# Linear attention with two gated networks: the low-half subtraction behind the state sums, and the out-projection written product by product

## The reference

```python
def linear_attention(x, Wq, Wk, Wv, Wo, out_norm_w):   # 8 heads of 128, chunks of 128 tokens
    def step(S, qkv):
        qb, kb, vb = qkv
        attn = jnp.einsum('bhid,bhjd->bhij', qb, kb)
        attn = jnp.where(causal, attn, 0.0)
        o = jnp.einsum('bhij,bhjv->bhiv', attn, vb) + jnp.einsum('bhid,bhdv->bhiv', qb, S)
        S = S + jnp.einsum('bhid,bhiv->bhdv', kb, vb)
        return (S, o)
    ...
    o = rmsnorm(o, out_norm_w)
    return o @ Wo
...
s = xn + linear_attention(rmsnorm(xn), ...)
s = s + silu(rmsnorm(s) @ Wgate) * (rmsnorm(s) @ Wup) @ Wdown
g = silu(fp4_network(xn))          # gate, up and down with 4-bit rounding in groups of 16
return x + s * g
```

## Time and profile before

| | us |
|---|---|
| median of 3 runs | 1060.57 |
| lowest, highest | 1059.28, 1060.98 |
| the profiled execution | 1059.62 |
| its span | 1057.9 |

### The profile page before, as it was taken

The page is one execution under the profiler, slowest core; times in us unless marked ns, Lnnn a source line. Parts: engine busy times, 40 slices in busy tenths (PEclk is TensorE's granted clock), DMA queues, the critical chain, the costliest instruction groups (busy, mean ns, idle before and its releaser), DMA issues.

```text
span 1057.9 us, 18981 instructions
## 1 busy us (share of the span) xinstructions
PE 1048.9 (99%) x6790; PEld 959.9 (91%) x6790; DVE 891.3 (84%) x1860; ACT 558.4 (53%) x1604; POOL 47.3 (4%) x68
## 2 busy tenths in 40 slices
PE   9999999999999999999999999999999999999998
PEld 6899999989999999998999989999999999999997
DVE  6788888888887888887777898889888888888887
ACT  6765765756757657667666634343333333333332
POOL 1000000000000000000000000101011010101010
PEclk9999999999999999999999999999999999999999
DMA  6555355455463553654446522253423233323213
GB/s 219 170 166 177 115 168 161 139 158 167 140 191 127 179 179 118 186 161 148 159 132 195 163 84 81 81 159 100 129 76 120 89 117 100 121 86 100 81 59 111
DMA packets 166238, 143.10 MB, mean 135 GB/s; under 512 B 28800, under 2 KB 162944, under 8 KB 166144
## 3 DMA queue, kind: packets, MB, share of 16 engines
q1 hardware_dynamic: 165456, 141.88, 43.2%
q10 hardware_dynamic: 688, 0.00, 0.0%
HBM read 77.27 MB, written 64.57 MB: 134 GB/s over the span
## 4 chain that ended last, share of the span: by engine, by line
PE 89%; DVE 4%; DMA 3%; ACT 2%; issue 1%; SPq 1%; DVEq 0%; ACTq 0%
PE ps L263 70%; PE ps L726 5%; PE ps L772 4%; PE ps L778 4%; PE ps L756 4%; DMA r_gate<-moved 1%; DMA moved<-work 1%; PE ps L861 1%; PE ps L614 0%; DMA work<-kept_w 0%; SPq L417 0%; DVE work L1406 0%; DMA work<-in_L_attn_hidden_states 0%; ACT work L996 0%; ACT work L969 0%
## 5 line engine op out<-in xcount | busy, mean ns | idle before, releaser
L263 PE MATMUL ps<-r_k,r_gate_up 128*128 128x512 f32 x768 | 185.2, 391 | 0.0
L263 PEld LDWEIGHTS ps<-r_k,r_gate_up 128*128 128x128 f32 x768 | 141.5, 188 | 27.2 <-DVE work L1654 0.4
L263 PE MATMUL ps<-r_o,onT 128*128 128x256 f32 x768 | 106.8, 288 | 0.0
L263 PE MATMUL ps<-r_h,r_k 128*128 128x512 f32 (+1 forms) x393 | 105.2, 403 | 0.0
L263 PEld LDWEIGHTS ps<-r_q,r_v 128*128 128x128 f32 x768 | 99.7, 191 | 4.9 <-DVE r_v L1658 0.3
L263 PE MATMUL ps<-r_q,r_v 128*128 128x256 f32 x768 | 102.3, 283 | 0.0
L969 ACT ACTIVATE work<-ps 128x128 f32<-128x128 f32 x256 | 67.1, 278 | 59.4 <-PE ps L778 59.2
L263 PE MATMUL ps<-r_h,r_q 128*128 128x512 f32 x384 | 98.2, 391 | 0.0
L263 PE MATMUL ps<-r_v,r_h 128*128 128x512 f32 x384 | 97.4, 390 | 0.0
L263 PEld LDWEIGHTS ps<-r_o,onT 128*128 128x128 f32 x768 | 95.7, 190 | 0.2
L1165 ACT ACTIVATE r_v<-work 128x512 fp32r<-128x512 f32 x64 | 40.5, 633 | 99.7 <-DVE work L1654 99.6
(11 more groups left out here) (161 smaller groups left out, 2049.3 us busy)
## 6 DMA issues: line engine op xcount, KB each, us to landing
moved<-work SPq DMA_DIRECT2D x63, 512.0 KB, 2.9
r_gate<-moved SPq DMA_DIRECT2D x252, 128.0 KB, 2.5
kept_h<-work SPq DMA_DIRECT2D x31, 384.0 KB, 2.6
work<-kept_h SPq DMA_DIRECT2D x124, 96.0 KB, 2.3
work<-in_L_attn_hidden_states SPq DMA_DIRECT2D x15, 512.0 KB, 5.1
kept<-work SPq DMA_DIRECT2D x9, 514.0 KB, 4.3
kept_h<-work SPq DMA_DIRECT2D x9, 512.0 KB, 3.5
kept_xq<-work SPq DMA_DIRECT2D x8, 512.0 KB, 5.4
```

The source lines that it names most:

```text
L263: done = pe.matmul(out_ap, a, b, start=first and n == 0, stop=last and n == 2, skip_group_check=skip)
```

## The change

On VectorE `o_lo` moves from ahead of the state sums to behind them, ahead of `late_extras`; only the very last step keeps its order. On TensorE the out-projection no longer goes chunk by chunk with three products each, but product by product with the four chunks each: high x high, then low weight x high activation, then high weight x low activation. It waits for `onT_hi` at its start and for `onT_ready` ahead of the last four matmuls.

```diff
@@ out_projection, tensor block
-                    pe.wait_ge(onT_ready, value)
-                    for c in range(CH):
-                        done = split_product(pe, ps[:, B_Y + c // 2, (c % 2) * D:(c % 2 + 1) * D],
-                                             lambda a: wo[:, a, h, :], lambda a: onT[:, a, c * P:(c + 1) * P],
-                                             "activation stationary", h == 0 and c % 2 == 0,
-                                             h == H - 1, skip=True)
+                    pe.wait_ge(onT_hi, value)
+                    for n, (wp, ap) in enumerate(((HI, HI), (LO, HI), (HI, LO))):
+                        if ap == LO:
+                            pe.wait_ge(onT_ready, value)
+                        for c in range(CH):
+                            done = pe.matmul(ps[:, B_Y + c // 2, (c % 2) * D:(c % 2 + 1) * D],
+                                             onT[:, ap, c * P:(c + 1) * P], wo[:, wp, h, :],
+                                             start=h == 0 and n == 0 and c % 2 == 0, stop=h == H - 1 and n == 2,
+                                             skip_group_check=True)
@@ attention, vector block
                     early_extras(b, j, mine)
                     if final and j == STEPS - 1:
                         last_o_lo(t0 + j - 1)
-                    elif not first or j >= LAG:
-                        o_lo(t0 + j - 1)
                     dve.wait_ge(ds_done, t0 + j + 1)
...
                         last = to
+                    if (not first or j >= LAG) and not (final and j == STEPS - 1):
+                        o_lo(t0 + j - 1)
                     late_extras(b, j, mine)
```

## The result

The changed kernel takes 1062.44 us (median; 1060.90 to 1064.59), the kernel before, in runs beside it, 1060.58 (1059.08 to 1062.86). The ratio of the two, formed from the means of these runs, is 1.0021 with a 95% interval of 1.0014 to 1.0028: slower, by 1.9 us from median to median and by 2.2 us from mean to mean. The interval lies on both sides of 0.2%, so the case is on the border between "within 0.2%" and "slower". The profiled execution took 1063.78 us, its span 1062.0.

A forecast was written before the change was run, and what follows sets the result against it. TensorE, busy 99% of the span, was taken as the bound, so only its standstills could be won. Gains of 1.95 us and losses of 3.3 gave +1.35, forecast 1061.9 us, range 1059.0 to 1064.0.

The forecast's parts named there:

- b1 j5: Batch 1, step 5 (steps 0 to 15, batches 0 to 3): sums start earlier without the subtraction ahead, 0.57 us won.
- b3 j4: Batch 3, step 4: TensorE's wait of 0.79 us for the sums shortened, 0.6 us won.
- b3 j12: Batch 3, step 12: the subtraction waiting for ScalarE's rounding no longer holds the sums, 0.58 us won.
- b0 j13: Batch 0, step 13: eight loads back from 1.18 to 0.97 us, 0.2 us won.
- b3 j14: Batch 3, step 14: counted at nothing, since VectorE then waits for ScalarE and a DMA; bounds 0 and 0.48 us won.
- Loss (a): j = 0 into j = 1, batches 1 to 3: VectorE 0.6 us late, all reaching TensorE; 1.8 us lost.
- Loss (b): j = 3 of each batch: next hidden state's low half late for the scores; 0.6 + 3 x 0.3 = 1.5 us lost.
- The price: VectorE time of the moved subtraction per step, start to next start: 0.6 us, bounds 0.57 and 0.69.
- full-duration rival: Subtraction costs its full duration, 0.69 us, and ScalarE's queue falls behind too: 1062.9 us, chance 0.22.
- Product order: TensorE's out-projection product by product: costed at nothing, 0.8 us either way; rival with its own price 1061.1 or 1062.7, chance 0.08.
- The ninth pair: Out-projection pair first needing the low half, ready 0.35 us before wanted; rival that it waits: 1065 us, chance 0.05.
- that lateness: VectorE's work after the moved subtraction, up to 0.6 us later; claimed never to add up, and hidden outside two step kinds.

The follow-up runs named there:

- the last experiment: Sums first only in j = 1, 5, 12, 13, 14, ScalarE's rounding behind the first state in j = 1; 1059.33 us against 1061.72 for the kernel before, ratio 0.9974.
- e2: Changed kernel, but in j = 0 of each batch the low-half subtraction stays ahead of the sums; 1061.75 us against 1060.95 for the kernel before, ratio 1.0002.
- e1: Kernel before with only the out-projection changed to product by product, the subtraction staying ahead of the sums; 1060.89 us against 1060.95, ratio 0.9996.
- e4: Changed kernel with the sums first only in j = 4, 5, 12, 13, 14; 1060.53 us, ratio 0.9994 to the kernel before.

## Why the prediction was right, and where it was not

**What bounds the kernel.** Right. The same instructions with gaps in other places give the whole difference.

**Gains.** The places were right, and so was the mechanism: no group at line 781 waits for the sums at b1 j5, b3 j4 and b3 j12 (the prediction had left a wait of about 0.2 at the first two). The size at the first two was too small, 0.57 and 0.6 where the table has 0.82 each. In the first profile of before, VectorE had waited for the exchange DMA at the transposed k of the same steps too, 0.54 at b1 j5 and 1.51 at b3 j4. I took these waits as fixed; in the other profiles of before they are shorter or absent (0 and 0.32 at b1 j5, 1.07 and 1.03 at b3 j4), and in after they are absent, so that the groups at line 781 are whole. Counted from the mean of three profiles of before the gain is 0.82, from the first one 1.02 and 1.13: the term was read from one profile of a place that varies. b3 j12 measured 0.52 for 0.58. b0 j13 was forecast as 0.2: two profiles of after win it, and so do the traces of the six other kernels with the sums first there and the new product order (0.17 to 0.20). The third of after loses 0.20, in an execution in which VectorE's transposes ahead of the sums end later, seen from TensorE; that, with 0.07 less in two profiles of before, brings the difference of the means to nothing. b3 j14, counted at nothing, is nothing net: what it wins is gone at j15, where the wait ahead of the gate products is 0.75 where the earlier trace rows has 0.22. Timeline after at j14 and j15:

```profile
589.29 1.69 DVE L1512 TENSOR_TENSOR r_gate<-work,r_gate 128x704 fp32r<-128x704 f32 x2 [0.96 <-ACT r_gate L1040]
...
592.30 0.94 PEld L263 LDWEIGHTS ps<-r_gate,r_k 128*128 128x128 f32 x6 [0.75 <-issue]
```

The VectorE row is that of the earlier trace rows for j14, where it waited 0.75: the sooner VectorE arrives, the longer it waits there.

**Loss (a).** 1.8 forecast, 1.9 measured, in all three profiles, and undone by the order of one step. Its form was as said too: a part already at the transposed k, the rest at the state products.

**Loss (b).** 0.6 + 3 x 0.3 = 1.5 forecast, 0.61 + 0.97 = 1.6 measured, and gone with j = 3 undone.

**The price.** 0.60, taken from the earlier trace rows and neighbours, is what the rows of b1 j0 show: 171.98 to 172.58. The full-duration rival (0.68 here) falls. By the Trainium skill ("VectorE: DVE Perf Modes", section "The DRAIN you can't avoid") the next operation waits until the pipeline has emptied, but the same section goes on that one which is not held starts earlier. The prediction left that out. This trace agrees with the second half: the next instruction starts 0.08 before the reported end, after as before. No new wait came up at j7 of the first halves either.

**Product order.** No price, 0.9996 with 0.0009 on either side. The ninth pair never waits: groups of twelve loads take 1.49 in the earlier trace rows and 1.50 in the rows of j3 above, and the list of waits has no line 1309 for TensorE. That the first halves cost nothing rests on it, as the run with VectorE's order alone shows at +20 us.

**What was missed.** The step that failed is "I followed that lateness through all steps by their rows". I followed it over VectorE, ScalarE and TensorE, to the transposed k of the same step, and not round by the exchange. SyncE's exchange of j5 carries the scaled output of VectorE and ScalarE together with the new k, and the scale factor stands behind the subtraction. So at b3 j5 the exchange leaves 0.57 us later after the scores, it lands later, and the transposed k of j6 is late. The rows at b3 j5 and j6 are those shown with the last experiment; the loss there is 0.57, and it takes back most of what b3 j4 wins. It is in all three profiles of after and in none of before, and in four of the five other kernels that have the sums first in j4 and the new product order (0.66, 0.49, 0.26, 0.50; 0.03 in the exception). The late exchange explains the first 0.57 of the transpose's 1.2 us of delay, measured from the scores of j5. The rest comes between the first read-back issue (line 417) and the transpose, 5.1 to 5.5 us in three profiles of before, 5.9 to 6.1 in those of after. Why that took longer is open. The exception (e2) shows that it matters: there the exchange leaves just as late, at 3.88, and TensorE is as early by the gain at b3 j4 (1.15), but the read-back takes 5.3, and only 0.03 is lost. So the late issue is one half of the cause, shown by the last experiment; it cost TensorE something only together with the longer transfer, and that half is not explained.

**How the total came out.** Terms forecast: -1.95 + 3.3 = +1.35. The same places as measured: -2.16 + 3.5 = +1.3. With b3 j6 it is +1.9, with the 0.28 of the second part, where the prediction had said that nothing moves, +2.2; the measured difference is 1.86 by medians and 2.2 by means. The forecast of the median was 0.5 us too low. Two losses of together 0.85 us were missing from it; that the rest came out so near is partly luck, since the larger gains and the larger losses cancel. What stays open is b2 j6 to j9: +0.5 of difference within a scatter of 1.5 in the kernel before. The exchange of b2 j5 leaves 0.57 later too, and undoing j = 4 took 0.7 off this place in one profile, so a part of it probably has the cause of b3 j6; one profile of a place with such a scatter doesn't show it.

## What to carry to other kernels

An instruction moved on a strictly ordered engine costs its distance to the next start, 0.60 here, but only in the steps that have no wait behind it to absorb it; two kinds of step out of sixteen decided the sign, and they can be found one by one in the trace of before. Where the order is written out per step, choose it per step: the edit in all steps lost 0.2%; in five chosen ones it made no difference clear of the noise (0.9994), and with a sixth, j1, and ScalarE's rounding moved there as well, it gained 0.2%. Lateness must be followed round by the DMA queue as well: ask which issue waits for the late engine, and who reads what it brings.

## What the runs showed of the hardware

- A stretch in which TensorE waits for a DMA exchange varies by up to 1.5 us between executions (b2 j6 to j9: 0, +0.92, +1.48 for the same kernel), while most steps repeat to 0.02. A difference of half a microsecond needs three profiles of each kernel, or it is one transfer's luck. The first profile of after, for example, has a wait at b0 j2, before the first step's moved subtraction has run, that the other two don't have (e1 and e4 have it too):

```profile
40.74 0.86 PEld L759 LDWEIGHTS ps<-work 128*128 128x128 f32 x7 [0.76 <-DVE work L1409]
```

- From the end of the awaited VectorE instruction to the load behind a separate wait in TensorE's sequencer it takes about 0.12 us: 56.61 after the end of line 1303 at 56.49 (55.09 + 1.40) at b0 j3, and 202.36 after 202.24 at b1. The same 0.12 stood in the earlier trace rows.
- The order in which a group of twelve 128x256 products goes over its PSUM areas had no effect that these runs can tell from noise, 0.9996 (0.9988 to 1.0005), though the area changes at each matmul.
